# Ordering of tokens in a mixture of experts: the slot one-hots move from VectorE to GpSimd

## The reference, cut to what matters

```python
gate_logits = x @ gate_w + gate_b
topk_vals, topk_idx = jax.lax.top_k(gate_logits, 2)
topk_w = jax.nn.softmax(topk_vals, axis=-1)
h = relu(einsum("bsh,ehf->bsef", x, w1) + b1)
expert_out = einsum("bsef,efh->bseh", h, w2) + b2
sel = take_along_axis(expert_out, topk_idx[..., None], axis=2)
moe = sum(topk_w[..., None] * sel, axis=2)
```

## Time and profile before

| what | value |
|---|---|
| median of three runs | 2781.92 us (2778.86 to 2784.38) |
| profiled execution, its own time | 2783.69 us |
| span of the profiled execution | 2782.1 us |
| PE busy | 2199.8 us (79%) |
| DVE busy | 1827.4 us (66%) |
| POOL busy | 1875.8 us (67%) |
| the loop over the groups, first L1503 to L1520 | 2226.63 to 2261.92 us, 35.3 us |

### The profile page before, as it was taken

The page is one execution under the profiler, slowest core; times in us unless marked ns, Lnnn a source line. Parts: engine busy times, 40 slices in busy tenths (PEclk is TensorE's granted clock), DMA queues, the critical chain, the costliest instruction groups (busy, mean ns, idle before and its releaser), DMA issues. The chain is left out here.

```text
span 2782.1 us, 54575 instructions
## 1 busy us (share of the span) xinstructions
PE 2199.8 (79%) x11643; PEld 1733.1 (62%) x11644; DVE 1827.4 (66%) x4373; ACT 931.7 (33%) x2267; POOL 1875.8 (67%) x1952
## 2 busy tenths in 40 slices
PE   5458777777777777478888888888888379999986
PEld 4346555555555555356666666666666279999975
DVE  5777777777777777476666666666666565555546
ACT  4323333333333333212222222222222144445436
POOL 3457777777777777567777777777777026666654
PEclk9789999999999999789999999999999689999998
DMA  7445555555555555466555555656565445555546
GB/s 230 140 126 148 146 148 144 145 147 145 147 146 146 147 146 135 114 214 165 156 157 162 156 162 154 161 156 162 156 163 151 104 114 102 103 105 105 101 86 191
DMA packets 261359, 402.24 MB, mean 145 GB/s; under 512 B 78916, under 2 KB 173531, under 8 KB 261276
## 3 DMA queue, kind: packets, MB, share of 16 engines
q0 software_dynamic: 103840, 258.38, 37.3%
q1 hardware_dynamic: 122376, 105.98, 14.2%
q10 hardware_dynamic: 35076, 37.13, 4.1%
HBM read 347.09 MB, written 54.62 MB: 144 GB/s over the span
## 5 line engine op out<-in xcount | busy, mean ns | idle before, releaser
L968 POOL DMA_INDIRECT gathered<-table,idx x1568 | 1491.1, 951 | 497.8 <-issue 451.5
L1299 PE MATMUL psA_e<-scaled,hotf 128*128 128x260 f32 x3136 | 745.4, 391 | 43.7 <-issue 38.8
L1299 PEld LDWEIGHTS psA_e<-scaled,hotf 128*128 128x128 f32 x3136 | 588.2, 193 | 131.6 <-issue 48.8
L1170 ACT ACTIVATE scaled<-t_e 128x32 f32<-128x32 f32 x196 | 45.0, 230 | 732.0 <-DVE t_e L1032 721.1
L1702 POOL DMA_INDIRECT moe_d<-xscaled,xtarget x113 | 179.9, 1592 | 121.5 <-DVE xtarget L1646 49.3
L1043 DVE TENSOR_TENSOR scaled<-gathered,psDW_e 128x2048 f32<-128x2048 f32 x98 | 223.7, 2282 | 25.8 <-ACT psDW_e L1171 25.8
L1036 DVE TENSOR_TENSOR hotf<-psA_e,code_r 128x1024 f32<-128x1024 f32 x196 | 239.7, 1223 | 0.0
L1043 DVE TENSOR_TENSOR scaled<-gathered,psW_e 128x2048 f32<-128x2048 f32 x98 | 223.6, 2282 | 21.2 <-ACT psW_e L1171 21.2
L1674 PEld LDWEIGHTS xpsH<-xxT,w1e 128*128 128x128 f32 x1808 | 221.2, 193 | 6.0 <-ACT xxT L1603 0.4
L1683 PE MATMUL xpsO<-w,hidT 128*128 x904 | 217.0, 383 | 6.3 <-DVE hidT L1635 6.0
L1674 PE MATMUL xpsH<-xxT,w1e 128*128 128x128 f32 x1808 | 221.9, 277 | 0.0
(11 more groups left out here) (338 smaller groups left out, 3381.1 us busy)
## 6 DMA issues: line engine op xcount, KB each, us to landing
w<-codes_d SPq DMA_DIRECT2D x196, 256.0 KB, 4.5
gathered<-table,idx POOLq DMA_INDIRECT x1592
w<-in_L_ffn_w ACTq DMA_DIRECT2D x8, 2048.0 KB, 20.6
xb<-in_L_ffn_b SPq DMA_DIRECT2D x113, 128.0 KB
table<-acc POOLq DMA_DIRECT2D x49, 130.0 KB
table<-acc ACTq DMA_DIRECT2D x49, 130.0 KB, 2.7
xnT_d<-w SPq DMA_DIRECT2D x49, 128.0 KB, 2.5
w<-xnT_d SPq DMA_DIRECT2D x49, 128.0 KB, 3.7
```

The source lines that it names most:

```text
L968: pool.indirect_dma_start(out=G[:, q, k, :], out_offset=None, in_=table, in_offset=bass.IndirectOffsetOnAxis(ap=idx[:, q, k:k + 1], axis=0 ...
L1170: act.activation(scaled[:, par, :, C:GW], t[:], ACT.Exp).then_inc(s["weights"], 1)
L1299: ins = pe.matmul(psA[:, q, 0:GW], hotf[:, q, k, :], scaled[:, par, k, :], start=(k == 0), stop=(k == KT - 1))
```

## The change

GpSimd makes the one-hots of the slots: one tensor_scalar of [128, 128] for each token tile and choice, which compares `across` with a scalar taken from `slot` in each partition. DVE keeps the one-hots of the tiles, one instruction a group. A new semaphore `rows` tells POOL that `slot` is written. `slots` now counts single instructions, and PE waits for two more of them before each token tile, where it waited once a group. The number and size of the buffers are as they were.

```diff
@@ gpsimd
+            pool.wait_ge(s["rows"], 1)
+            for g, group in enumerate(groups):
+                if g >= 2:
+                    pool.wait_ge(s["listed"], groups[g - 2][-1] + 1)
+                for m, i in enumerate(group):
+                    for k in range(2):
+                        pool.tensor_scalar(slots[:, g % 2, 2 * m + k, :], across, slot[:, i, k:k + 1], None, ALU.is_equal).then_inc(s["slots"], 1)
@@ vector
             chain.link(dve.tensor_copy(slot, part_i[:]))
+            dve.sem_inc(s["rows"], 1)
...
-                for into, width, at, told in ((places, XT, tile, "places"), (slots, P, slot, "slots")):
-                    dve.tensor_tensor(into[:, g % 2, 0:n, :], across[:, 0:width].rearrange("p (m f) -> p m f", m=1).to_broadcast([P, n, width]),
-                                      at[:, lo:hi, :].rearrange("p t (k f) -> p (t k) f", f=1).to_broadcast([P, n, width]), ALU.is_equal).then_inc(s[told], 1)
+                dve.tensor_tensor(places[:, g % 2, 0:n, :], across[:, 0:XT].rearrange("p (m f) -> p m f", m=1).to_broadcast([P, n, XT]),
+                                  tile[:, lo:hi, :].rearrange("p t (k f) -> p (t k) f", f=1).to_broadcast([P, n, XT]), ALU.is_equal).then_inc(s["places"], 1)
@@ tensor
             for g, group in enumerate(groups):
-                pe.wait_ge(s["slots"], g + 1)
                 for m, i in enumerate(group):
                     r = rows_of(i)
                     pe.wait_ge(s["tokens"], i + 1)
+                    pe.wait_ge(s["slots"], 2 * i + 2)
```

More of the change, by code:

```diff
@@ L1419, in order @@
         s = {n: sem("o_" + n) for n in ("consts", "steps", "both", "ranked", "pads", "slots", "places", "tokens", "listed", "b1", "b1T", "extra",
-                                        "upto", "column", "past", "owner")}
+                                        "upto", "column", "past", "owner", "rows")}
         block = ctx.enter_context(nc.Block())
```

## The result

| | before | changed |
|---|---|---|
| median | 2781.93 us (2778.86 to 2784.38, 4 runs) | 2822.71 us (2819.05 to 2826.43, 4 runs) |
| span of the profiled execution | 2782.1 us | 2822.5 us |
| loop, first places instruction to the work on psL | 35.3 us | 65.1 us |

The ratio is 1.0138, 95% interval [1.0123, 1.0153]. The prediction said 2806.5 us, 2786 to 2842, slower with 0.88.

A forecast was written before the change was run, and what follows sets the result against it. DVE bounds the loop at full clock, then POOL: from 2233.85 us, 43.0 us for 86 instructions, 9.0 for 15 collisions and 0.7 hand-over give 2286.55, +24.6 us. Forecast 2806.5 us, range 2786 to 2842.

The forecast's parts named there:

- What bounds the loop: In the 35.3 us loop: PE limits up to 2238 us, DVE from 2242 us on at 1.70 us a group.
- The price of a POOL instruction: Each of the 98 POOL tensor_scalar in the loop was taken at 0.50 us from one start to the next.
- 0.555 by my sum: Duration of one 128-column POOL instruction: L964's 0.49 us for 49 columns plus 79 columns at 0.00083 us.
- The collisions: DVE's 17 places instructions, with two SBUF operands, hold POOL up in the loop: 0.6 us each, 10.2 us in all.
- The pair of L964: Evidence for collisions: L964 took 0.49 us undisturbed, 0.69 us where a 0.37 us DVE tensor_tensor had started 0.03 us earlier.
- The hand-over at the end: After POOL's last instruction, PE's last token tile (0.47 us) and two handovers of about 0.1 us: 0.7 us.
- Costed at nothing: PE's waits at each token tile, the wait for `rows`, ACT and PE's clock, hidden under POOL's 3.6 us a group.
- The one that ends faster: Rival: cheap POOL instructions in the loop, t = 0.24 us without collisions, gain 4.3 us, 2777.6 us; chance 0.11.
- Its bound from PE: With slots free of cost, PE would limit the loop, L1520 starting at 2257.6: a gain of 4.3 us at most.
- The rival without collisions: As forecast in the loop, but POOL and DVE do not collide: +15.5 us, 2797.4 us; chance 0.17.
- The dear rival: POOL's columns in the loop costly or comparison slow, t = 0.87 us: +60.9 us, 2842.8 us; chance 0.14.
- The forecast proper: POOL paces the loop, t from 0.40 to 0.65 us with collisions: +16 to +39 us, 2798 to 2821; chance 0.45.

The follow-up runs named there:

- the run without collisions: Changed kernel with the places instruction's operand `tile` kept in PSUM, one SBUF operand instead of two: 2812.99 us, ratio 1.0114 to the kernel before.
- the comparisons alone: Kernel before plus 98 one-column POOL comparisons behind the stage's constants that nobody waits for: ratio 1.0035 to the kernel before.
- the repeated runs: Both kernels run again without edits: the kernel before 2782.63 us, ratio 1.0007; the changed one 2818.44 us, ratio 1.0137.

## Why the prediction was right, point by point

- **What bounds the loop.** Right: DVE before, POOL after, and the whole loss of the loop passes on to the end (the stretch from L1520 to the next stage is 2.2 us in both). The forecast of what the profile would show was less good. PE was to stand idle before each token tile with POOL as releaser, and "if PE or ACT still releases most of the waits" was a sign of being wrong. By the view that is what happened: it puts PE's waits down to ACT (PEld 19.3 us) and DVE's to PE (43 us), and names POOL once. The starts of the weight loads, 0.11 us behind every second POOL instruction, show that POOL is the releaser all the same.
- **The price of a POOL instruction.** I took 0.50 us from one start to the next; it is 0.58 undisturbed. The duration, 0.555 by my sum, was 0.595. The overlap of 0.05 us that I took off, from memset and iota, is 0.02 or less. The reasoning behind 0.555 was wrong in both its parts (some 0.23 us for the fetch and 0.83 ns a column; measured 0.08 us and 2.2 to 2.6 ns a column). L964 was some 0.09 us too dear a start, since a comparison of 49 columns takes about 0.40 us (an estimate between its 0.31 us for 8 columns and 0.44 for 64) and not 0.49. The 79 further columns cost 0.19 us and not 0.07. That these errors nearly cancelled was luck. 98 x 0.08 = +7.8 us on the sum.
- **The collisions.** Real, and priced too high: 0.41 us each and not 0.60, 6.9 us and not 10.2: -3.3 us. The guess that part of a POOL instruction may run meanwhile was right: its first 0.13 us. What the price lacked is that DVE's instruction begins inside a POOL instruction that runs on undisturbed, which covers another 0.21 to 0.37 us. The pair of L964 fits the same reading: DVE's instruction ended at 1168.34, L964 at 1168.69, 0.35 us later, which is its 0.49 less 0.14.
- **The hand-over at the end.** 1.4 us and not 0.7, because PE works at clock 0.50 there and I had reckoned with 1.00: +0.7 us.
- **The loop.** 24.6 + 7.8 - 3.3 + 0.7 = 29.8 us, which is what the profile shows.
- **Costed at nothing.** PE's waits, ACT and the clock: right but for the clock in the last 1.4 us, as the run without collisions shows. What I had not priced is the second pass over the edges, +5.2 us in the profiles and reproduced by instructions that no one waits for. "An earlier or later stage has changed its length by more than a microsecond or two" was my own sign of a wrong prediction, and it is what happened.
- **The rivals.** The one that ends faster fell: one instruction costs 0.58 us from start to start where it needs less than 0.32, and even one of 8 columns costs 0.285. Its bound from PE held up: with a third of the slots on POOL and no collisions the loop gains 1.6 to 3.9 us, where I had 4.3 at most. The rival without collisions is the kernel with `tile` in PSUM, whose loop is 22.9 us longer than before where the rival had 15.5, mostly for the price of POOL's instruction (98 x 0.08 us). The dear rival (5.5 ns a column) had the right idea, that columns are dear, and twice their price. The Trainium skill's "roughly line-rate" for one-input work on GpSimd ("GPSIMD Engine Reference", "Engine selection") is not what these rows show: 2.6 ns a column, against DVE's 952 ns for 768 columns, 1.2 ns a column with its fixed part.
- **The total.** Of +40.4 us between the profiles, 29.8 are the loop, 5.2 the second pass, which the comparisons alone come near to, and 5.4 the other stages, where the repeated runs show scatter. The second set of runs had +36.6 us. The forecast proper, 2798 to 2821 us, missed the measured 2822.71 by little, with its loop inside its terms and the rest outside of them; the wider range held because it made room for dearer POOL instructions, not for the second pass.

## What to carry to other kernels

Moving work to an idle engine pays only if that engine can do it within the pace that the stage has now: here 0.28 us an instruction, against 0.58. Price such an instruction in its own form and width before moving it, since the rows of its neighbours (memset, affine_select, a 49-column tensor_scalar) gave 0.24 to 0.87. If POOL must read SBUF beside DVE, move one operand of DVE's two-operand instructions to PSUM, which gave 6.9 us in this loop. And before believing the releaser that a view names, compare the starts with the ends of every engine that is waited for. Compare the stages that were not touched, not only the total.

## What was not expected of the hardware

- In a collision POOL loses and DVE hardly does. POOL's instruction is held until DVE's is over, all but 0.13 us, even where POOL had been in steady work before. With a third of the slots on POOL, DVE runs two such instructions back to back, and the POOL instruction beside them takes 1.5 to 1.9 us (1103 ns on average with the undisturbed ones, against 604 with the operands in PSUM). DVE's places instruction took 902 ns on average in that kernel and 858 with its operand in PSUM.
- DVE instructions with one SBUF operand were also stretched beside POOL. In the changed kernel's loop, where POOL was busy throughout:

```profile
L1523 DVE TENSOR_SCALAR xbefore_i<-acc 1x113 int32<-1x113 f32 x2 | 0.8, 418 | 0.1
L1524 DVE TENSOR_SCALAR xbefore_i<-xbefore_i 1x113 int32<-1x113 int32 x2 | 0.8, 404 | 0.1
```

  Both took 207 ns in the kernel before. The repeated run has it again (387 and 537 ns, 208 and 544). A busy POOL alone does not do it: with `tile` in PSUM POOL is just as busy, and the four take 208 to 266 ns. What makes the difference stays open. They are off the path here.
- 98 tensor_scalar instructions further down in POOL's program go with a median of 953 ns in place of 946 for the gathers of an earlier loop, and 0.3% on the kernel; 32 of them, in the two kernels with a third of the slots, go with 953 and 957 ns.
